# ScalarE takes the delta's larger-than-zero part and the expert layernorm's moments, in two passes with sums kept

## The reference, cut to what matters

```python
def rat_write(res, y, ...):                      # once after attention, once after the MLP
    out, delta_low = o_d[..., :H], o_d[..., H:]  # H = 512
    delta = softplus(delta_low @ du_w.T + du_b)
    A_neg = -softplus(A_logit)
    A_bar = exp(delta * A_neg)
    B_bar = (A_bar - 1.0) / (A_neg - SSM_EPS) * B_proj
    return hs * A_full + out * B_full
def ffn(x, A, B, Wr, br):                        # x is _layernorm(x): mean and variance over 2048
    scores = 8 * softmax(x @ Wr.T + br)
    low = einsum('bsd,hrd->bshr', x, A)
    return 2 * einsum('bshr,hor,bsh->bso', low, B, scores)
x = x + attention_and_mlp_layer(_layernorm(x))
x = x + ffn(_layernorm(x))
```

## Time and profile before

| | us |
|---|---|
| runs shown | 1856.93, 1858.18, 1860.12 |
| median of the three | 1858.18 |
| profiled execution, its own time | 1859.11 |
| span of the core in the profile | 1857.3 |
| granted TensorE clock, mean | 0.939 of full speed |

### The profile page before, as it was taken

The page is one execution under the profiler, slowest core; times in us unless marked ns, Lnnn a source line. Parts: engine busy times, 40 slices in busy tenths (PEclk is TensorE's granted clock), DMA queues, the critical chain, the costliest instruction groups (busy, mean ns, idle before and its releaser), DMA issues.

```text
span 1857.3 us, 23597 instructions
## 1 busy us (share of the span) xinstructions
PE 1648.2 (89%) x8854; PEld 1138.3 (61%) x8854; DVE 1173.0 (63%) x1873; ACT 794.4 (43%) x1486; POOL 267.6 (14%) x243
## 2 busy tenths in 40 slices
PE   6799999999999866899898999897999998999865
PEld 5565655666666535677566677455677565775543
DVE  6678755888888657254355647637458455555577
ACT  1333336888887634455224444223444322331221
POOL 1235332334320000200002000003000002000000
PEclk7899999999999976799898999998999999999988
DMA  7376567878775252566473666554565544665721
GB/s 301 114 266 239 209 172 232 242 205 243 213 195 119 71 203 96 187 223 205 147 236 127 228 214 202 173 164 169 190 234 196 191 161 149 222 200 173 252 79 68
DMA packets 117221, 348.69 MB, mean 188 GB/s; under 512 B 16226, under 2 KB 33250, under 8 KB 101876
## 3 DMA queue, kind: packets, MB, share of 16 engines
q1 hardware_dynamic: 117108, 347.19, 57.6%
HBM read 271.37 MB, written 75.76 MB: 187 GB/s over the span
## 4 chain that ended last, share of the span: by engine, by line
PE 65%; DVE 22%; ACT 6%; issue 4%; DMA 1%; POOL 1%; SPq 0%; DVEq 0%; ACTq 0%
PE ps L1365 15%; PE ps L1377 11%; PE ps L396 6%; PE ps L820 4%; PE ps L1280 4%; PE ps L807 4%; PE ps L843 4%; PE ps L1323 3%; PE ps L1265 3%; PE ps L1308 3%; ACT a_p L922 3%; PE ps L1335 2%; DVE m_A L1438 2%; PE ps L369 2%; DVE m_A L1469 2%
## 5 line engine op out<-in xcount | busy, mean ns | idle before, releaser
L1365 PE MATMUL ps<-m_yhi,m_win 128*128 128x512 f32 x1024 | 352.9, 413 | 0.0
L1377 PE MATMUL ps<-m_wod,m_hT 128*128 128x512 f32 (+1 forms) x1024 | 312.2, 454 | 8.0 <-DVE m_hT L1563 8.0
L1377 PEld LDWEIGHTS ps<-m_wod,m_hT 128*128 128x128 f32 x1024 | 173.6, 201 | 152.0 <-issue 151.5
L1365 PEld LDWEIGHTS ps<-m_yhi,m_win 128*128 128x128 f32 x1024 | 195.4, 191 | 49.2 <-issue 5.1
L864 DVE TENSOR_REDUCE a_negmax<-ps 128x1 f32<-128x640 f32 (+7 forms) x176 | 180.6, 1026 | 59.6 <-PE ps L810 58.7
L1365 PE MATMUL ps<-m_ylo,m_win 128*128 128x512 f32 x512 | 203.9, 398 | 0.0
L922 ACT ACTIVATE a_p<-ps,a_negmax 128x128 f32<-128x128 f32 (+7 forms) x256 | 188.8, 750 | 30.4 <-DVE a_negmax L864 28.0
L820 PE MATMUL ps<-ident,a_p 128*128 128x128 f32 x1152 | 157.5, 275 | 1.4 <-DVE a_pT L877 1.2
L1595 ACT ACTIVATE m_turned<-ps 128x512 f32<-128x512 f32 x128 | 74.0, 593 | 187.8 <-PE ps L1265 187.7
L807 PE MATMUL ps<-a_k,a_q 128*128 128x512 f32 (+3 forms) x384 | 124.2, 403 | 17.1 <-ACT a_p L922 15.3
L820 PEld LDWEIGHTS ps<-ident,a_p 128*128 128x128 f32 x1152 | 123.7, 141 | 3.3 <-DVE a_pT L877 1.9
(11 more groups left out here) (202 smaller groups left out, 2730.4 us busy)
## 6 DMA issues: line engine op xcount, KB each, us to landing
m_win<-mlp_in_split SPq DMA_DIRECT2D x128, 512.0 KB, 4.2
m_wod<-in_wod2T SPq DMA_DIRECT2D x128, 316.0 KB, 3.1
m_wod<-in_wod1T SPq DMA_DIRECT2D x64, 316.0 KB, 3.1
p_xT<-in_xT SPq DMA_DIRECT2D x16, 1024.0 KB, 9.1
p_x<-in_x SPq DMA_DIRECT2D x16, 1024.0 KB, 10.5
a_q<-qk_split SPq DMA_DIRECT2D x64, 256.0 KB, 6.4
a_k<-qk_split SPq DMA_DIRECT2D x128, 128.0 KB, 7.0
mlp_in_split<-a_w_two SPq DMA_DIRECT2D x32, 512.0 KB, 3.0
```

Source lines behind the costliest of these rows:

```text
L1365: m = nc.tensor.matmul(bank_of("m", blk, step), win[s][:, wl, ic, :], y[:, k, :], start=(ic == 0 and p3 == 0), stop=(ic == HCH - 1 and p3 ...
L1377: m = nc.tensor.matmul(ps[:, b, 0:cn], hT[:, k, P * q:P * q + P], w2[s][:, c0:c0 + cn], start=(k == 0), stop=(k == MCH - 1))
```

## The change

Three things move. The larger-than-zero part of the delta becomes a second activation on ACT, right behind the absolute value, so that one reader (ACT) frees the bank, and DVE's `delta` part is gone. The moments of the experts' layernorm go from DVE to ACT: part `stats`, still at 8.5, is now Identity over the 2048 values with the sum kept, a small activation that makes the negative mean, and Square with that as bias and the sum kept. Both wide passes write a result that nobody reads into the buffer `m_x`, from which the input was added. POOL divides by D, adds EPS and takes the power. The load of the next input into `m_x` waits for `evar_ready` in place of `x2_ready`, and `stats` waits also for `elw_ready` of the tile four back, whose moments had the same buffer. The two buffers `e_stats` are gone.

```diff
@@ -227,7 +227,6 @@
         oTt = sb("m_oT", [P, HCH, P])
         low = [sb("e_low0", [P, EW + NE])]
         m_st = sb("m_stats", [P, TB, RD2, 2, 6])
-        e_st = [sb(f"e_stats{k}", [P, 4, 6]) for k in range(2)]
         e_mv = [sb(f"e_moments{k}", [P, 8]) for k in range(4)]
         start = place[0]
         identb = sb("a_identb", [P, P], BF16)
@@ -1169,10 +1168,8 @@
             if what == "a" and part == "wod":
                 one.plan((what, i, "out"), pair if first else None)
                 one.plan((what, i, "ab"), pair + 1 if first else None)
-            if what in "aw" and part == "low":
+            if what in "aw" and part in ("low", "delta"):
                 one.plan((what, i, part))
-            if what in "aw" and part == "delta":
-                one.plan((what, i, part), readers=2)
             if what in "ae" and part == "turn":
                 one.plan((what, i, "turn", q))
             if what == "a" and part == "read" and q % 2 == 0:
@@ -1419,13 +1416,7 @@
                 dve.wait_ge(memsets_done, LOWS_SET)
                 V.tensor_copy(dlT[k][0:DR, :], ps[0:DR, one.bank((what, i, "low")), 0:P]
                               ).then_inc(one.sem((what, i, "low")), 1)
-            if part == "delta":
-
-                dve.wait_ge(one.sem((what, i, "delta")), one.before((what, i, "delta")) + 1)
-                V.tensor_scalar(delta[k][:, :], bank_of(what, i, "delta"), 0.0, None, ALU.max).then_inc(
-                    one.sem((what, i, "delta")), 1)
             if part == "gates":
-                wait_for_emptied(dve, what, i, "delta")
                 dve.wait_ge(soft_ready, 2 * nth("delta", what, i) - 1)
                 dve_own.then_inc(V.tensor_tensor(delta[k][:, :], delta[k][:, :], tmp[k][:, :], ALU.add))
                 dve.wait_ge(soft_ready, 2 * nth("delta", what, i))
@@ -1498,15 +1489,6 @@
         def expert_dve(i, part, q):
             X, m, s = hs[hs_of["w", i]], e_mv[i % 4], i % 2
             r = e_rt[s]
-            if part == "stats":
-                dve.wait_ge(x2_ready, i + 1)
-                for a in range(4):
-                    c = dve_own.then_inc(V.bn_stats(e_st[s][:, a, :], X[:, 512 * a:512 * a + 512]))
-                dve.wait_ge(dve_own.sem, c)
-                c = dve_own.then_inc(V.bn_aggr(m[:, 0:2], e_st[s][:, :, :]))
-                dve.wait_ge(dve_own.sem, c)
-                dve_own.then_inc(V.tensor_scalar(m[:, 2:3], m[:, 0:1], -1.0, None, ALU.mult))
-                V.tensor_scalar(m[:, 3:4], m[:, 1:2], EPS, None, ALU.add).then_inc(evar_ready, 1)
             if part == "router":
                 dve.wait_ge(quarter_used, quarter["e", i, 3] + 1)
                 dve.wait_ge(evar_ready, i + 1)
@@ -1606,8 +1588,10 @@
             if part == "delta":
                 act.wait_ge(delta_mm, nth("delta", what, i))
                 act.wait_ge(skip_ready, nth_before("scale", what, i))
-                S.activation(tmp[k][:, :], bank_of(what, i, "delta"), ACT.Abs).then_inc(one.sem((what, i, "delta")), 1)
-                act.wait_ge(one.sem((what, i, "delta")), one.before((what, i, "delta")) + 1)
+                n = act_own.then_inc(S.activation(tmp[k][:, :], bank_of(what, i, "delta"), ACT.Abs))
+                S.activation(delta[k][:, :], bank_of(what, i, "delta"), ACT.Relu).then_inc(
+                    one.sem((what, i, "delta")), 1)
+                act.wait_ge(act_own.sem, n)
                 n = act_own.then_inc(S.activation(tmp[k][:, :], tmp[k][:, :], ACT.Exp, scale=-1.0))
                 act.wait_ge(act_own.sem, n)
                 S.activation(tmp[k][:, :], tmp[k][:, :], ACT.Ln, bias=1.0).then_inc(soft_ready, 1)
@@ -1647,6 +1631,17 @@
                 m.then_inc(one.sem((what, i, "read", 1)), 1)
 
         def expert_act(i, part, q):
+            if part == "stats":
+
+                X, m, spare = hs[hs_of["w", i]], e_mv[i % 4], m_x[x_place(i)]
+                act.wait_ge(x2_ready, i + 1)
+                act.wait_ge(elw_ready, i - 3)
+                n = act_own.then_inc(S.activation(spare[:, :], X[:, :], ACT.Identity, accum_out=m[:, 0:1]))
+                act.wait_ge(act_own.sem, n)
+                n = act_own.then_inc(S.activation(m[:, 2:3], m[:, 0:1], ACT.Identity, scale=-1.0 / D))
+                act.wait_ge(act_own.sem, n)
+                S.activation(spare[:, :], X[:, :], ACT.Square, bias=m[:, 2:3],
+                             accum_out=m[:, 1:2]).then_inc(evar_ready, 1)
             if part == "turn":
                 keep_quarter("e", i, q)
             if part == "router":
@@ -1713,6 +1708,8 @@
             if part == "stats":
                 m = e_mv[i % 4]
                 pool.wait_ge(evar_ready, i + 1)
+                n = pool_own.then_inc(G.tensor_scalar(m[:, 3:4], m[:, 1:2], 1.0 / D, EPS, ALU.mult, ALU.add))
+                pool.wait_ge(pool_own.sem, n)
                 G.tensor_tensor(m[:, 4:5], m[:, 3:4], mhalf[:, 0:1], ALU.pow).then_inc(erstd_ready, 1)
 
         def turn_pool(blk, k):
@@ -1775,7 +1772,7 @@
                     sp.wait_ge(mlp_mm, 32 * NBLK)
                 earlier = [j for j in range(i) if x_place(j) == x_at]
                 if earlier:
-                    sp.wait_ge(x2_ready, earlier[-1] + 1)
+                    sp.wait_ge(evar_ready, earlier[-1] + 1)
                 move(m_x[x_at][:, :], x[i]).then_inc(mx_loaded[x_at], 16)
             if part == "turn" and q == 0:
                 sp.wait_ge(hs_ready, nth("sum", what, i))
```

## The result

The changed kernel takes 1874.03 us (median of 4 runs, 1872.93 to 1876.36), the kernel before beside it 1859.15 us (1856.93 to 1860.83). The ratio is 1.0082, its 95% interval 1.0065 to 1.0100: slower by 14.9 us, where 32 had been forecast. Its profiled execution spans 1872.1 us at a mean granted clock of 0.941 (before: 1857.3 us, 0.939).

A forecast was written before the change was run, and what follows sets the result against it. The prediction took PE, 89% busy, as the bound, with ACT's queue stopping it at six tiles. Terms 26.0 + 8.7 + 1.9 - 2.2 - 0.6 - 1.1 = 32.7 us gave a forecast of 1890 us, range 1866 to 1906.

The forecast's parts named there:

- What bounds the kernel, and the mechanism: PE, busy 89% of the span, sets the end and has no reserve beside tile 1 against a later ACT.
- Removed and added work: DVE loses 70 us; ACT gains 4.85 us a tile, 78 us in all, its 32 second activations costed at nothing.
- lower bound of 4.4 us: Cost of `stats` per tile on ACT if a pass without two per-partition operands is some 0.2 us shorter.
- Tiles 1, 2, 5, 6: Up steps with an "a" tile beside: each loses 4.5 us of waiting and 2.0 of clock, 26.0 us slower together.
- rival 2: Same stops, mostly absorbed: no clock cost, later short waits take part in; about 1868, a loss of 10, chance 0.11.
- Tiles 9, 10: Up steps without an "a" tile: PE stops 2.65 us plus 1.7 of clock at each, 8.7 us slower together.
- Tiles 3, 7, 11: Down steps without a Silu: later kept quarter costs 0.85 us at tiles 3 and 7, 0.2 at 11; sum +1.9.
- Tiles 0, 4, 8: Step 56 on: kept quarter 2.1 us earlier at tile 4, tile 0 alike, tile 8 2.0 us later; together -2.2.
- First tiles and the end: One maximum off the path in the first write-backs, -0.6 us; tile 15's first product earlier at the end, -1.1 us.
- The sum: Whole kernel: all terms add to 32.7 us slower, say 32 on the profiled 1859.1; forecast 1890 us.
- all bounds low: Whole kernel with 4.4 us a tile on ACT and no clock loss: about 14 us slower, 1872.
- Rival 3: Faster, relief of DVE decides at steps 56 on and the end: some 27 us gained if passes are hidden, 1831; chance 0.08.

The follow-up runs named there:

- e3: The changed kernel with the moments on ACT at list place 13.6 instead of 8.5, behind the kept quarters: 1837.95 us, ratio 0.9885 to the kernel before.
- e1: The kernel before with only the delta part of the change, the moments staying on DVE at 8.5: 1852.99 us, ratio 0.9967 to the kernel before.
- e2: The changed kernel with the delta part turned back, so only the moments move to ACT: 1881.10 us, ratio 1.0121 to the kernel before.
- e10: The kernel before with only the place of the moments, on DVE, changed from 8.5 to 13.6: 1837.96 us, ratio 0.9878.
- e6: The kernel before with the delta part and the moments, still on DVE, at 13.6 instead of 8.5: 1835.62 us, ratio 0.9875.
- e7: The changed kernel without the second wide pass (squares), so outputs differ from the reference's: 1851.30 us, ratio 0.9969 to the kernel before.
- e9: The changed kernel, unchanged, traced a second time: span 1875.3 us.

## Why the prediction was right in sign and too high

**What bounds the kernel, and the mechanism: right.** PE has no reserve there against a later ACT, and the stops came where the prediction put them: Silus 5.7 us behind the end of x, 1.11 us for bank 0 and 2.61 us for the kept quarter, the product 12.1 us behind x (12.7 said). e3 shows that nothing else holds the loss.

**Removed and added work: nearly right.** DVE 1107.7 us busy (1103 said), ACT 872.0 (890 said). The passes were the first term that was too high: 1.92 and 2.01 us and two reads of 0.18 and 0.19, 4.38 us a tile from the first start to the table load, against 4.85. The nearest row, 2.10 us, has two per-partition operands; the one with none is 0.19 us shorter, the one with one 0.10. The rule of the Trainium skill (ScalarE: Activation LUTs, What ACT_TABLE_LOAD costs) had given 1.89 and 1.99 us and an estimate of 4.5 us a tile, and the trace agrees with it to 0.02 us a pass in the median. The lower bound of 4.4 us was the right one.

**Tiles 1, 2, 5, 6: the step that failed, +26.0 said, +19.7 and +18.3 measured.** Its term was 4 x (4.5 + 2.0). The waiting was 3.7 us a tile, not 4.5 (14.9 in all, 18.0 said): 0.5 of the difference is the shorter passes, the rest smaller steps on the way to the first kept quarter. The clock was priced at a flat 2.0 after each stop, 8.0 in all. In the first trace tiles 1 and 5 lost it (5.3 and 5.5 us with the waiting) and tiles 2 and 6 hardly (3.9 each), in the second only tile 5: 3.7 and 2.3 us in all. So the term was about 4 x 3.7 and one or two times 1.7. The whole step was too high by 6 to 8 us, most of it clock. That a stop could cost no clock stood in the prediction as a bound (0 to 2.7), and in rival 2 as a case for all stops at once; the mixture wasn't.

**Tiles 9, 10: right.** 2 x 3.9 measured, 2 x 4.35 said; the difference is the pass time.

**Tiles 3, 7, 11: small, wrong sign.** +1.9 said, about -0.7 measured for 3 and 7. I priced the later kept quarter (2.15 to 2.82 us of waiting, 0.7 against the 0.85 said) and left out that PE's transposes ahead of it wait for x itself, which comes earlier by the maximum removed (1.00 to 0.53 us).

**Tiles 0, 4, 8: gains too low.** -2.2 said, -5.9 and -7.3 measured, though 3.7 of that is within what before differs from itself. At tile 4 the gain isn't where I put it. The kept quarter's wait did not shrink (3.39 us); the wait of 2.70 us for the delta's maximum did, which I had overlooked, with part of it returned in the next wait. e1 and e2 show the column at -1.9 and -3.5, so both parts may hold some of it. At tile 8 I had forecast a loss of 2.0: PE did stop 3.9 us for ACT there, but other waits went, and the place came out at +0.3.

**First tiles and the end.** -0.6 and -1.1 said. The -4.3 of the first trace up to 966 us did not repeat, it was +1.6 in the second, so it belongs to one execution. The end is -1.8 in both.

**The sum.** e2 gives the moments alone a cost of 22 us and e1 the delta part a gain of 6; the prediction had no gain of that size for the delta part. Of the 18 us between forecast and result in the ledger, 6.3 are tiles 1, 2, 5, 6, 0.9 tiles 9 and 10, 2.4 tiles 3 and 7, 3.7 tiles 0, 4, 8, 3.7 the first tiles and 0.9 the end. In the second trace, 14.7 us from the forecast, tiles 1, 2, 5, 6 are 7.7 and tiles 0, 4, 8 are 5.1, and the first tiles count 2.2 the other way. So the step above is the largest in both, and beside the first tiles all errors point the same way: I priced stops at the full and gains only where I had looked for them. The prediction's price with all bounds low is close to the +14.9 of the medians, in part by luck: its passes were right, and gains made up for the clock that was lost. It is given as +14; its own terms add up to about 16 (and those with all bounds high to about 43, not 47).

**The rivals.** Rival 2 (1868) is in part true: the stops were not absorbed, but two of the six cost hardly any clock in the first trace and three in the second. Rival 3 was right that there is a gain once the passes are out of the way, and wrong about its cause. It put the gain at 27 us if the passes were hidden, and e3 hides them and gets 21. But e10 gets the same 21 with the moments on DVE, so what PE gains is that nothing stands between x and the gates, not that DVE is relieved. The prediction quoted the Trainium skill (Perfetto Trace Analysis, Optimizing Scalar/DVE Operations) for moving work to Scalar when DVE is saturated. No run bears that out for the moments here: 45 us less on DVE (e6 against e3) is worth nothing that can be measured. For the delta's larger-than-zero part it fits: e1 gains 6 us.

**What stays open.** Which stops lose the clock: e7's shorter stops lost it at all four tiles, the change's longer ones, which come in two pieces, at two or one. How much of the column of tiles 0, 4, 8 is the change's own. And by which waits the delta part gains its 6 us.

## What to carry to other kernels

Before work is moved to a less busy engine, look at what stands behind it in that engine's queue and at when its input comes: here the wait for x (6.6 us idle) held up Silus that could have run. And ask first who reads the result and when: the moments' first reader is some 20 us behind x, and moving them there is worth 17 to 22 us with the moments on DVE (e1 to e6, before to e10) and 36 with them on ACT, while moving them to ACT at the early place costs 21. A stop of PE is its wait plus, sometimes, 1.5 to 1.8 us of clock, so price several stops as a mixture with a spread, not at one value each.

## What the runs showed of the hardware

- A ScalarE pass over 128x2048 with its sum kept took 1.91 us without per-partition operands (14 alike, 1.89 to 1.92), 2.00 with one and 2.10 with two; keeping the sum adds a separate read of 0.18 to 0.19 us.
- Equal stops of PE (1.11 and 2.61 us) were followed by a granted clock of 0.50 in one execution and 1.00 in the next, at the same tile. Eight products took 2.18 us in the one and 1.20 us in the other.
- A shorter stop can lose more clock: beside tile 1 one wait of 2.08 us in e7 cost 3.6 us, 1.5 beyond the wait, and two waits of 3.7 us together in e9 cost 3.9, 0.2 beyond.
- Two executions of the same kernel stood 1.7 (before) and 3.1 us (the change) apart at 760 us, 2.6 and 5.9 us apart at 966 us, and 1.7 and 3.2 us apart at the end.
